# Four layers of graph message passing: three tiles a layer fetched row by row instead of five, and seven tiles gathered on TensorE in every middle step

## What is computed

```
for l in range(4):
    e   = edge_weight * We[l] + be[l]                      # per edge, 512 wide
    m   = relu(x[src] + e)
    agg = segment_sum(m, dst)                              # edges -> nodes
    h   = ((1 + eps[l]) * x + agg) @ W1[l] + b1[l]
    h   = relu(batch_norm(h, over the nodes) * gamma[l] + beta[l])
    x   = relu(h @ W2[l] + b2[l])
out = layernorm(x_in + x)
```

## Time and profile before

| | us |
|---|---|
| median of 3 timed runs | 1928.99 (1920.86 to 1932.24) |
| the profiled execution | 1921.04 |
| its span | 1919.2 |
| TensorE matmul busy (PE) | 1399.5 (73%), 7507 instructions |
| VectorE busy (DVE) | 1293.6 (67%), 2331 |
| POOL busy | 978.0 (51%), 1038 |
| ScalarE busy (ACT) | 273.9 (14%), 651 |
| DMA issues of row tiles by SP | 1536 + 1024, of 2 KB |

### The profile page before, as it was taken

The page is one execution under the profiler, slowest core; times in us unless marked ns, Lnnn a source line. Parts: engine busy times, 40 slices in busy tenths (PEclk is TensorE's granted clock), DMA queues, the critical chain, the costliest instruction groups (busy, mean ns, idle before and its releaser), DMA issues.

```text
span 1919.2 us, 25205 instructions
## 1 busy us (share of the span) xinstructions
PE 1399.5 (73%) x7507; PEld 802.4 (42%) x7507; DVE 1293.6 (67%) x2331; ACT 273.9 (14%) x651; POOL 978.0 (51%) x1038
## 2 busy tenths in 40 slices
PE   1568888879658878872955878887295678888648
PEld 0244555445325544441532545454153344545324
DVE  7967778767467776762647768676354867777547
ACT  1200101105101100010510100010050000011004
POOL 4455665560656666661065666556106556666600
PEclk9979988889878989995987999898597889999869
DMA  6556665553655666662265666665226556666613
GB/s 228 160 165 174 170 174 167 155 170 115 203 146 170 178 175 183 172 182 69 87 200 162 177 180 176 169 176 169 62 98 197 169 155 180 175 178 176 181 51 120
DMA packets 105657, 306.84 MB, mean 160 GB/s; under 512 B 21826, under 2 KB 22978, under 8 KB 105516
## 3 DMA queue, kind: packets, MB, share of 16 engines
q0 software_dynamic: 82240, 269.55, 49.2%
q1 hardware_dynamic: 23276, 35.62, 5.8%
HBM read 292.29 MB, written 12.80 MB: 159 GB/s over the span
## 4 chain that ended last, share of the span: by engine, by line
SPq 40%; issue 28%; PE 26%; DVE 5%; DMA 1%; DVEq 0%; ACT 0%
SPq L607 33%; PE y_ps L1860 6%; SPq L601 6%; PE y_ps L1711 6%; PE pair_ps L1664 6%; PE h_ps L1813 3%; DVE rows L1278 1%; PE uT_ps L1766 1%; PE uT_ps L1759 1%; PE uT_ps L1773 1%; DVE rows L1262 0%; PE uT_ps L1748 0%; DVE pair_sb L1205 0%; PE h_ps L1640 0%; PE pair_ps L1799 0%
## 5 line engine op out<-in xcount | busy, mean ns | idle before, releaser
L695 POOL DMA_INDIRECT rows<-node_table,src_fast x972 | 918.6, 945 | 704.0 <-issue 263.0
L1278 DVE SCALAR_TENSOR_TENSOR rows<-We_ps,negw_fast,rows 128x512 f32<-128x512 f32 x1028 | 700.3, 740 | 0.4
L1664 PE MATMUL pair_ps<-rows,onehot 128*32 128x512 f32 x2504 | 415.0, 692 | 309.3 <-DVE rows L1278 196.7
L1711 PE MATMUL y_ps<-table_parts,src_onehot 128*128 128x512 f32 x1632 | 490.3, 438 | 19.0 <-issue 18.0
L1711 PEld LDWEIGHTS y_ps<-table_parts,src_onehot 128*128 128x128 f32 x1632 | 310.1, 204 | 328.9 <-issue 263.9
L1278 DVE SCALAR_TENSOR_TENSOR rows<-We_bc,negw_fast,y_ps 128x512 f32<-128x512 f32 x204 | 151.5, 743 | 312.3 <-remote 176.1
L1664 PEld LDWEIGHTS pair_ps<-rows,onehot 128*32 128x32 f32 x2504 | 60.7, 114 | 437.6 <-issue 243.2
L1813 PE MATMUL h_ps<-uT,W_sb 128*128 128x128 f32 x1152 | 158.0, 297 | 70.2 <-issue 69.9
L1813 PEld LDWEIGHTS h_ps<-uT,W_sb 128*128 128x128 f32 x1152 | 149.9, 211 | 86.7 <-issue 85.8
L847 ACT COPY pair_sb<-pair_ps 128x512 f32<-128x512 f32 x76 | 44.3, 582 | 783.8 <-remote 407.5
L1096 DVE TENSOR_TENSOR src_onehot<-y_ps,src_bc 128x512 fp32r<-128x512 f32 x204 | 138.5, 680 | 0.0
(11 more groups left out here) (201 smaller groups left out, 887.3 us busy)
## 6 DMA issues: line engine op xcount, KB each, us to landing
be_bc<-node_table SPq DMA_DIRECT2D x1536, 2.0 KB
b_bc<-node_table SPq DMA_DIRECT2D x1024, 2.0 KB
rows<-node_table,src_fast POOLq DMA_INDIRECT x972
node_table<-rows SPq DMA_DIRECT2D x29, 256.0 KB, 2.0
x_now<-x_pad SPq DMA_DIRECT2D x10, 512.0 KB, 6.4
W_sb<-W SPq DMA_DIRECT2D x4, 1024.0 KB
rows<-W SPq DMA_DIRECT2D x16, 256.0 KB, 2.7
out<-rows SPq DMA_DIRECT2D x8, 256.0 KB
```

The source lines that it names most:

```text
L695: nc.gpsimd.indirect_dma_start(rows[:, slot, :], None, source, bass.IndirectOffsetOnAxis(places[:, t:t + 1], 0)).then_inc(landed[q], 16)
L1278: last = nc.vector.scalar_tensor_tensor(rows[:, slot, :], We_of, negw_fast[:, t:t + 1], row, ALU.mult, ALU.max)
L1664: last = nc.tensor.matmul(pair_ps[h][WIN * win:WIN * (win + 1), :], onehot[:, h, tile - h * PAIR, :], rows[:, slot, :], start=t in firsts, ...
L1711: last = nc.tensor.matmul(y_ps[k % 2][:, :], src_onehot[:, first + at, :], table_parts[:, part, at, :], start=(part, at) == PLACES[0], sto ...
```

## The change

The list of row tiles becomes [2, 4, 6], and the quads with a tile gathered on TensorE become the same seven in all middle steps.

```diff
-    BY_ROW = [1, 3, 5, 7, 8]
+    BY_ROW = [2, 4, 6]
     ROW_TILE = STEP - 1
...
     def pe_quads(l, i):
-        return () if i not in SORTED else (0, 1, 2, 3, 4, 6) if i in BY_ROW else (0, 1, 2, 3, 4, 5, 6)
+        return tuple(range(USED_RUNS)) if i in SORTED else ()
```

## The result

The changed kernel takes 1802.96 us (median of four runs, 1790.45 to 1812.37), the kernel before 1925.6 beside it: a ratio of 0.9357, with an interval of 0.9279 to 0.9434. By the medians that is 122.6 us less, by the two profiled executions 110.2 (1921.04 and 1810.87). Forecast were 86 by the profiled execution and 1837 us, with a range of 1798 to 1874.

What follows compares the result with a forecast made beforehand. SP's row-by-row fetches, 40% of the chain, were taken as the bound, with VectorE waiting at step 8. Terms -90.3 - 18 + 24 + 0 + 1 - 3 gave -86 us; forecast median 1837 us, range 1798 to 1874.

Steps and rivals of the forecast that it cites:

- Point 1: Row fetches move to steps 2, 4, 6; SP leaves the path and three waits at step 8 go: -90.3 us.
- Point 2: VectorE's row waits at earlier steps, 36.1 us, go too, but part was won back afterwards: -18 us, bounds 10 and 36.
- Point 3: Steps 1, 3, 5, 7, 8 gather seven tiles on TensorE, not six: 20 more at 1.2 us each, +24 us.
- Rival (a): TensorE becomes the bound; added tiles cost 54 to 80 us instead of 24: about 1865 to 1893 us; chance 0.13.
- rival (c): Slower: VectorE waits for the 20 added gathered tiles; from 5.6 us each all gains are eaten; chance 0.02.
- Point 4: POOL does 12 gathers less of 0.93 us, beside other work: 0; if POOL were the bound, 11 us gained.
- Point 5: Preparation: two row-number loads fewer, one more group of index rows spread (a matmul group and a copy): +1 us.
- point 6: TensorE starts slow after the wait; without the gap a few groups a layer run at full clock: -3 us.
- Layer 0: Without row waits, this layer shows the price of the gathered tiles alone: 4 to 11 us longer.
- Rival (b): Steps run faster once SP is off the path, at 35.4 us: about 1795 us, at best 1780; chance 0.09.
- (d): SP stays on the path because a fetch runs later than its step: some 1870 to 1890 us; chance 0.03.
- (e): Row fetches are hidden in truth, something else ends at the same moment: 1946 us; chance 0.01.

Runs made afterwards that it cites:

- t9: Kernel before with no row tile in step 8, which gathers seven tiles on TensorE instead; chip B: 1807.6 us, ratio 0.950.
- t10: Changed kernel, but steps 1, 3, 5, 7 and 8 gather six tiles on TensorE and POOL fetches the seventh; chip B: 1809.1 us, 0.950 of before.
- n8: Changed kernel without any row tile (BY_ROW empty), POOL fetching 25 tiles in each of steps 1 to 8; chip A: 1772.7 us, 0.922 of before.
- e1: Changed kernel with row tiles back in steps 1, 3, 5, 7 and 8, seven gathered tiles kept; chip C: 1474.0 us, 0.988 of before.
- r5: The changed kernel as it is, timed again beside the kernel before, on chip A: 1807.5 us, ratio 0.937.
- s6: Kernel before with four empty SP instructions ahead of each row's DMA, which left fetches no longer; chip A: 1921.7 us, ratio 0.9985.
- the unread fetches: Changed kernel with two more row fetches a layer that nobody reads: 1479.7 us on chip C (0.993 of before), 1478.9 on D (0.994).

## Why the prediction was right, point by point

*What bounds the kernel.* Right for the chip it was read from. The chain, SP's timeline and VectorE's waits named the place, and t9 shows it: one entry taken from the list gives 94.9 us of 1902.4, where the whole change gave 118.9 of 1926.4 on chip A.

*Point 1, -90.3 us.* Right. Step 8 became 86.2 us shorter in the three layers, SP left the chain, no row tile is waited for. The margin at step 6 of layer 1 was 26 us, not 41: the third fetch began 5 us later than I had it (the first took 103 us and not 98), took 78 us and not 71, and its tile was used 4 us earlier.

*Point 2, -18 us.* The mechanism I named (waits are won back by the next steps) was right, and by t9 and t10, on one chip, it goes further than half: 75 us of such waits stand in the trace of t9, and layers 1 to 3 are 0.8 us longer than without them. The two pairs of before and after leave more room: beyond the waits at step 8 layers 1 to 3 lost 23 us in the first pair and 11.7 on chip A. Part of that can be the two fetches fewer in each layer (three fewer gave 10.6 us in n8, so by that rate, an estimate, 7); it was not separated. My upper bound, 36, had no basis in what follows a wait; the row of 70.8 us for two steps said so already. I had also counted only the waits put down to row DMAs: three more, of 9.3 us together, stand under "issue" at the same multiplies (two of them in the earlier trace rows, 4.76 and 1.40). The sign that steps 2 to 7 become alike came half true: they last 32.5 to 42.2 us, before 31.0 to 44.4.

*Point 3, +24 us.* This is the term that failed. On the long-fetch chips no run shows such a price: t10, without the 20 tiles, is not 24 us faster but, by its ratio, slower. That the price is nothing is not shown either, as said at t10. I took 1.2 a tile, between a comparison of two steps with two, whose lengths vary by 2 us from one to the next, and a mean wait. On the short-fetch chips layer 0 shows 0.5 to 1.0 us a tile, near my lower bound of 0.76. That TensorE and VectorE took the added work into time in which they were idle is the plain reading, but it was not shown by itself. Rival (a), TensorE as the bound, and rival (c), late tiles, fall by the result: layer 0 became 7.5 us shorter, not longer, and the mean wait for a gathered tile went from 1.53 to 1.40 us. The Trainium skill's "Perfetto Trace Analysis", section "Identifying the Most-Contended Engine", warns against taking matmul busy time for the distance to the limit. The traces agree: 32 to 35 of some 40 us were no limit here, nor were 175.55 of 183.0 in e1.

*Point 4, 0 for POOL.* Not contradicted where steps take 37 us, but no run there changes POOL's fetches alone, and t10's ratio leaves room for 0.75 us each. On the short-fetch chips POOL sets the pace from layer 1 on, and a fetch is worth 1.3 us there.

*Point 5, +1 us, and point 6, -3 us.* Neither can be seen: the time ahead of layer 0 differs by 13 us between r5 and n8, and by 4.6 between the kernel before and s6, more than both terms.

*Layer 0.* I forecast +4 to +11 us as the bare price of the tiles; it is -7.5 (and -11.7 on chip A). That is the sign that I had wrong. Layer 0 has no row waits, so something else than waiting for rows became less. Two fetches fewer is the only large thing removed there, and n8 points the same way, but t9 doesn't fit the row, and the test made for it (the unread fetches) met a chip where it can't show. It stays open.

*The sum.* By the pair on chip A the change is worth 109.7 us: 83.9 of waiting at step 8 (the three waits of s6), 11.7 more in layers 1 to 3, 11.7 in layer 0, and 2.4 elsewhere. The forecast had 90 + 18 + 3 - 25. It missed 24 us. That 24 is also what I had put on the tiles is partly luck: for layers 1 to 3 my terms sum to 93 (three quarters of the tiles), against 95.6 measured on A, and 113.4 in the first pair. On A most of what was missed lies in layer 0, where I had 6 us more and 11.7 less came. So the number came out right by a right first term and by errors of some 10 to 20 us whose places differ from pair to pair. Rival (b), a faster pace once SP is off, gave nearly the number (1795) for a wrong reason: steps 2 to 7 take 37.1 to 37.3 us on the mean of a layer, near the 37.8 that I took, not 35.4. Rivals (d) and (e) fell: the fetches are early, and with them the waits are gone.

That the result depends on the chip was in none of my cases. Had the kernels been timed on C or D, where they take less than 1500 us, the range would have missed by some 300 us. That both were timed on a long-fetch chip was luck.

## What to carry to other kernels

Look for the place where a periodic supply meets two consumers in a row: five fetches of 75 us against steps of 37 only hurt where two fetches were needed one step apart, and removing that one need gave most of the gain (94.9 us in t9, and t10 no more). Waits that the following steps win back are worth little, however many microseconds they sum to (75 in t9); check what the next step's length does before counting them. And if the bound is the issue rate of an engine, time both kernels on more than one chip before tuning the rest.

## What the runs showed of the hardware

Chips differ by 29% for the same kernel (1926 and 1488 us), with the same durations of single instructions: an indirect DMA on POOL takes 0.945 to 0.948 us, a multiply on VectorE 0.740 to 0.746, on either kind. The granted clock of TensorE goes between the same two levels, 1.2 and 2.4 GHz, but its mean differs: 0.85 to 0.88 of 2.4 GHz in the kernel before on A, 0.93 to 0.96 on C. Whether that is a cause of the longer time or comes of TensorE's being idle more often there was not tested. What differs besides is how instructions follow each other. On the short-fetch chips 90% of SP's row DMAs come 0.28 to 0.36 us after the one before; on the long-fetch ones 23 to 31% do. Some follow there within 0.15 us, but many come after 0.70, 1.4 or 2.1 us, so that the mean is 0.61 to 0.64 instead of 0.40. TensorE shows it too. In the changed kernel, in the product with W1 of layer 0's step 8, matmuls come in ones and twos, 0.7 or 1.4 us apart. The whole product of step 8 takes 9.0 us there, and 3.7 in e1:

```profile
411.97 0.39 PE L1813 MATMUL h_ps<-uT,W_sb 128*128 128x128 f32 x2 [1.03 <-issue]
412.71 0.27 PE L1813 MATMUL h_ps<-uT,W_sb 128*128 128x128 f32 x1 [0.34 <-issue]
414.13 0.27 PE L1813 MATMUL h_ps<-uT,W_sb 128*128 128x128 f32 x1 [1.15 <-issue]
414.85 0.37 PE L1813 MATMUL h_ps<-uT,W_sb 128*128 128x128 f32 x1 [0.45 <-issue]
416.96 3.42 PE L1664 MATMUL pair_ps<-rows,onehot 128*32 128x512 f32 x8 [1.73 <-issue]
```

Over the run, this is TensorE's idle time ahead of the matmuls of this product (last number: all of it, then what is put down to "issue"), in the kernel before and in e1; in the changed kernel it is 36.8 us:

```profile
L1813 PE MATMUL h_ps<-uT,W_sb 128*128 128x128 f32 x1152 | 158.0, 297 | 70.2 <-issue 69.9
...
L1813 PE MATMUL h_ps<-uT,W_sb 128*128 128x128 f32 x1152 | 137.3, 278 | 0.0
```

Such idle time is put down to "issue", that is to nothing the profile shows, and on VectorE it was absent from the same place when other instructions were taken out (n8). What makes a chip one or the other was not found; nothing in one core's trace tells it.

Of the kernels timed, the best depends on the kind. On chip A it is the one without any row tile, 1772.7 us against 1807.5 for the changed one; on C and D the one with five row tiles and seven gathered ones, 1474.0 and 1471.8. Neither was timed on the other kind.
